# One table set for Ln and Exp, y normalised by ScalarE, and a new issue order in the six local-attention layers of a Trainium2 kernel

## The chip, the cores and the metric

The kernel runs on one core of a Trainium2 chip. The metric is device time in microseconds (us) of one execution. The engines are named as in the profile: PE is TensorE (PEld its weight loads), ACT is ScalarE, DVE is VectorE, POOL is GpSimd and SP is SyncE, which issues the DMAs.

## What is computed

Two blocks, each with a residual, on x of shape (4, 1024, 128). The first is causal attention with relative positions (16 heads of 8). The second, to which the change belongs, is six layers of local attention and a gated feed-forward net. In outline (shift_tokens moves half of the channels down by one token; a layernorm stands around each block):

```python
def attn_layer(x, Wqkv, qs, ksc, Wo):
    q, k, v = split_heads(x @ Wqkv)                 # 16 heads of 64
    q, k = l2norm(q) * qs, l2norm(k) * ksc
    q, k = rotary(q, k)                             # tables of cos and sin, times a scale
    out = local_attention(q, k, v)                  # windows of 32: own and the one before, softmax
    return out @ Wo

def ffn_layer(x, g, bln, W1, b1, W2, b2):
    xn = (x - mu) / sqrt(var + 1e-5) * g + bln
    a, gate = split(xn @ W1 + b1)                   # 341 columns each
    return a * gelu(gate) @ W2 + b2

for i in range(6):
    x = attn_layer(shift_tokens(x), ...) + x
    x = ffn_layer(shift_tokens(x), ...) + x
```

## The kernel before, in words

`build` runs five parts, one after the other: `first_projections`, `first_attention`, `first_output`, `layers` and `last_output`. Only `layers` changes. It treats the 4096 tokens as 32 tiles of 128 tokens; six layers make 192 tiles (TILES), numbered n, and m is the place of a tile in a ring of 8. Every engine has its own program: a function `body(t)` that lists the operations of that engine in the order of issue, where `for n, m in t.back(5)` names the tile that is five tiles behind the newest. So one body is a software pipeline over seven tiles, written out by hand. `rounds` writes the first 8 bodies out, then a loop (Fori) of 23 turns with 8 bodies in each, then the bodies that drain the pipeline (DEEPEST of them). Engines wait for each other by semaphores (a Mark each), and each engine issues strictly in its own order, so what is queued behind a waiting instruction waits too.

The work of one tile, by the engine that does it (lines are those of the kernel before):

- POOL copies the tile of x (`x_copied`, L964), PE turns it (`turn_x`, L1317), ACT copies it out of PSUM (`x_turned`, L1188 and L1189).
- PE computes q, k and v in six matmuls of 512 columns (`qkv`, L1328) into two PSUM banks in turn. Of the four pieces of q and k, ACT takes squares (`squared`, L1194), DVE sums them (`squares`, L1060) and multiplies with the rotary tables (`turned`, L1053); the two of v are copied by ACT (`v_out`, L1201).
- The l2 norm: DVE clips the sums (`clipped`, L1066), ACT guesses 1/sqrt as exp(-0.5 ln(s)) (`guess`, L1207 the Ln, L1209 the Exp), POOL makes one Newton step (`newton`, L984 to L990) and scales (`scaled`, L995), after it added the two halves of the rotation (`added`, L978 and L979).
- PE transposes q and k (`turn_q` L1336, `turn_k` L1343), ACT copies them out (`q_turned` L1216 and L1217, `k_turned` L1226), in two halves each. PE makes the scores (L1361), DVE subtracts the maximum, ACT takes the exponential (`exp`, L1231), DVE sums and normalises, PE transposes (`turn_p`, L1369), ACT copies out (`p_turned`, L1237 and L1238), PE multiplies with v (`values`, L1384) and ACT copies out (`o_out`, L1243).
- `out_proj` (PE, L1392), `with_x` (DVE), a shift by a DMA (`y_shifted`), `stats` (DVE), the root by POOL (`root`, L119), then `one`: DVE subtracts the mean and multiplies with 1/std (L124). PE turns the result (`turn_y`, L1398), ACT copies it out with gain and bias (`y_turned`, L1249).
- The feed-forward net runs once for two tiles, in bodies with an odd place: for each of three pieces PE computes value and gate (`hidden`, L1410), ACT the gelu of 256 columns (`gelu`, L1256), DVE the product (`gated`, L1115). Then `back_out` (PE, L1420) and `next_x` (DVE).

ScalarE computes Ln, Exp and Gelu from tables. Copy, Square and Identity are in every set of tables. The builder puts a table load (ACT_TABLE_LOAD) in front of a function that the set loaded last does not hold: in the kernel before these are in front of the Ln (L1207), the Exp of the guess (L1209), the first Gelu after an Exp (L1256) and the first Exp after a Gelu (L1231). A load that the program asks for itself stays where it is written.

Of the kernel before, what the change touches and what calls it, by code (L numbers as in the profile page):

```python
# [8 lines left out]
ALU = mybir.AluOpType  # L9
# [25 lines left out]
EPS = 1e-5  # L35
TILES = DEPTH * NT
# [4 lines left out]
DEEPEST = 7  # L41
# [773 lines left out]
def layers(nc, a, X, ident):  # L815

    with Part(nc, "la") as t:
# [19 lines left out]
        oT, yn, ynT = t.sb("oT", [P, 8, P]), t.sb("yn", [P, E]), t.sb("ynT", [P, 2, 2 * P])  # L837
        Y, yb = t.sb("Y", [P, TB + 1, 3 * (E // 2)]), t.sb("yb", [P, 4, E])
# [19 lines left out]
        wo_mm, y_ev, yn_ev, nT_mm, nT_ev, yb_ev = (mark(n) for n in ("wom", "ye", "yn", "ntm", "nte", "yb"))  # L858
# [26 lines left out]
        def _(e):  # L885
# [46 lines left out]
            def body(t):  # L932
                for n, m in t.back(7):
                    next_layer(n, m)
                for n, m in t.back(6):
                    w1_in(n, m)
                for n, m in t.back(5):
                    y_shifted(n, m)
                for n, m in t.back(3):
                    v_shifted(n, m)  # L940
# [5 lines left out]
        def _(e):  # L946
# [69 lines left out]
            def body(t):  # L1016
                for n, m in t.back(0):
                    x_copied(n, m)
                for n, m in t.back(1):
                    table(n, m)  # L1020
                for n, m in t.back(4):
                    added(n, m, 0)
                    added(n, m, 1)
                    carried(n, m)
                    newton(n, m)
                for n, m in t.back(6):
                    with_b2(n, m)
                for n, m in t.back(4):
                    scaled(n, m, 0)
                for n, m in t.back(6):  # L1030
                    root(n, m)
                for n, m in t.back(4):
                    scaled(n, m, 1)
# [3 lines left out]
        def _(e):  # L1037
            for mark in (x_ev, ss_ev, rot_ev, cl_ev, sub_ev, nm_ev, y_ev, yn_ev, a_ev, c_mx, c_sum, c_rc):
                mark.open(e)
# [85 lines left out]
            def body(t):  # L1125
                for n, m in t.back(5):
                    over_sum(n, m, 0)
                    normal(n, m, 0)
                    largest(n, m, 1)
                    below(n, m, 1)  # L1130
                for n, m in t.back(6):
                    stats(n, m)
                for n, m in t.back(3):
                    turned(n, m, 0)
                for n, m in t.back(7):
                    if m % 2:
                        gated(n, m, 2)
                for n, m in t.back(5):
                    summed(n, m, 1)
                for n, m in t.back(6):  # L1140
                    one(n, m)
                for n, m in t.back(3):
                    squares(n, m, 0)
                    turned(n, m, 1)
                for n, m in t.back(5):
                    over_sum(n, m, 1)
                    normal(n, m, 1)
                for n, m in t.back(3):
                    squares(n, m, 1)
                    turned(n, m, 2)  # L1150
                for n, m in t.back(4):
                    largest(n, m, 0)
                for n, m in t.back(6):
                    if m % 2:
                        gated(n, m, 0)
                for n, m in t.back(3):
                    turned(n, m, 3)
                for n, m in t.back(4):
                    below(n, m, 0)
                for n, m in t.back(3):  # L1160
                    squares(n, m, 3)
                    squares(n, m, 2)
                    clipped(n, m)
                for n, m in t.back(6):
                    if m % 2:
                        gated(n, m, 1)
                for n, m in t.back(4):
                    summed(n, m, 0)
                for n, m in t.back(7):
                    if m % 2:  # L1170
                        next_x(n, m)
                for n, m in t.back(5):
                    with_x(n, m)
# [3 lines left out]
        def _(e):  # L1177
            for mark in (xT_ev, sq_ev, v_ev, r_ev, c_ln, Tq_ev, Tk_ev, ex_ev, pt_ev, o_ev, nT_ev, g_ev):
# [66 lines left out]

            def y_turned(n, m):
# [12 lines left out]
            def body(t):  # L1259
                for n, m in t.back(7):  # L1260
                    if m % 2:
                        gelu(n, m, 2)
                for n, m in t.back(5):
                    exp(n, m, 1)
                for n, m in t.back(0):
                    x_turned(n, m)
                for n, m in t.back(3):
                    squared(n, m, 1)
                for n, m in t.back(5):
                    p_turned(n, m, 0)  # L1270
                for n, m in t.back(4):
                    q_turned(n, m, 0)
                for n, m in t.back(6):
                    y_turned(n, m)
                for n, m in t.back(5):
                    o_out(n, m, 0)
                for n, m in t.back(4):
                    k_turned(n, m, 0)
                for n, m in t.back(3):
                    squared(n, m, 2)  # L1280
                for n, m in t.back(5):
                    p_turned(n, m, 1)
                for n, m in t.back(3):
                    squared(n, m, 3)
                for n, m in t.back(6):
                    if m % 2:
                        gelu(n, m, 0)
                for n, m in t.back(4):
                    q_turned(n, m, 1)
                for n, m in t.back(5):  # L1290
                    o_out(n, m, 1)
                for n, m in t.back(3):
                    v_out(n, m, 4)
                for n, m in t.back(6):
                    if m % 2:
                        gelu(n, m, 1)
                for n, m in t.back(4):
                    exp(n, m, 0)
                    k_turned(n, m, 1)
                for n, m in t.back(3):  # L1300
# [7 lines left out]
        def _(e):  # L1308
# [115 lines left out]
            def body(t):  # L1424
                for n, m in t.back(0):
# [4 lines left out]
                for n, m in t.back(3):  # L1430
                    qkv(n, m, 1)
                for n, m in t.back(4):
                    e.wait_ge(Tk_ev.sem, Tk_ev.v(n - 1, 2))
                    e.wait_ge(Tq_ev.sem, Tq_ev.v(n - 1, 2))
                    turn_q(n, m, 0)
                for n, m in t.back(3):
                    qkv(n, m, 2)
                for n, m in t.back(7):
                    if m % 2:
                        back_out(n, m)  # L1440
                for n, m in t.back(6):
                    e.wait_ge(xT_ev.sem, xT_ev.v(upto(n + 6)))
# [3 lines left out]
                for n, m in t.back(5):  # L1446
                    e.wait_ge(pt_ev.sem, pt_ev.v(n, 1))
                    e.wait_ge(o_ev.sem, o_ev.v(n - 1, 2))
                    values(n, m, 0)
                for n, m in t.back(4):  # L1450
                    e.wait_ge(Tq_ev.sem, Tq_ev.v(n, 1))
                    e.wait_ge(Tk_ev.sem, Tk_ev.v(n - 1, 2))
                    turn_k(n, m, 0)
                for n, m in t.back(3):
                    qkv(n, m, 3)
                for n, m in t.back(5):
                    e.wait_ge(o_ev.sem, o_ev.v(n, 1))
                    e.wait_ge(pt_ev.sem, pt_ev.v(n, 1))
                    turn_p(n, m, 1)
                for n, m in t.back(6):  # L1460
                    if m % 2:
                        hidden(n, m, 0)
                for n, m in t.back(4):
                    e.wait_ge(Tk_ev.sem, Tk_ev.v(n, 1))
                    e.wait_ge(Tq_ev.sem, Tq_ev.v(n, 1))
                    turn_q(n, m, 1)
                    scores(n, m, 0)
                for n, m in t.back(5):
# [3 lines left out]
                for n, m in t.back(3):  # L1472
                    qkv(n, m, 4)
                for n, m in t.back(6):
# [158 lines left out]
```

## Time and profile before

| | |
|---|---|
| time, median of 3 runs | 5648.67 us (5640.5 to 5655.38) |
| the profiled execution's own time | 5650.0 us |
| its span in the profile | 5648.2 us |
| PE busy (matmuls) | 4771.1 us, 84% |
| ACT busy | 4267.2 us, 76% |
| DVE busy | 3970.2 us, 70% |
| POOL busy | 2332.2 us, 41% |
| mean granted TensorE clock | 0.948 of full speed |

Busy time is the time in which an engine has at least one instruction under way; the span is that of the profiled execution from its first to its last instruction. Shares are averages over parts of the program that differ: the layers take some seven tenths of the span.

### The profile page before, as it was taken

The numbers are of one execution on the slowest core, as the hardware profiler recorded it, in microseconds if no ns is written. First come the engines' busy times: TensorE is split into PE (matmuls) and PEld (weight loads), VectorE is DVE, ScalarE is ACT, GpSimd is POOL, SyncE is SP. The second block draws the span as 40 slices with busy tenths as digits, with TensorE's granted clock in tenths as the row PEclk, the third lists the DMA queues.
The fourth block names the chain that finished last, engine by engine and source line by source line (L and its number), as shares of the span: only waits on it lengthen the run. The fifth ranks groups of instructions, "written<-read, shape, count | busy, mean of one in ns | idle before, by whom it ended". The sixth has DMA issues, their size and how long they took to land. (4 is left out here: it accounts for less than half of the span.)

```text
span 5648.2 us, 139360 instructions
## 1 busy us (share of the span) xinstructions
PE 4771.1 (84%) x44000; PEld 3074.7 (54%) x44000; DVE 3970.2 (70%) x9123; ACT 4267.2 (76%) x7350; POOL 2332.2 (41%) x2840
## 2 busy tenths in 40 slices
PE   4999999999588888888888888888888888888884
PEld 2444444444355665556565655666556556665563
DVE  5666666656677777777777777777777777777774
ACT  1555555555288888888888888888888888888883
POOL 0000000000255555555555555555555555555552
PEclk6999999999699999999999999999999999999996
DMA  6444444444111111111111111111111111111111
GB/s 218 144 135 145 138 145 145 132 138 143 65 37 37 37 28 34 37 37 33 37 36 32 31 37 37 37 34 31 34 37 33 37 37 36 27 35 37 37 36 39
DMA packets 258979, 361.58 MB, mean 64 GB/s; under 512 B 44404, under 2 KB 216156, under 8 KB 257884
## 3 DMA queue, kind: packets, MB, share of 16 engines
q1 hardware_dynamic: 258140, 351.55, 20.3%
q8 instruction: 386, 6.32, 0.5%
q14 instruction: 453, 3.71, 0.2%
HBM read 151.19 MB, written 93.34 MB: 43 GB/s over the span
## 5 line engine op out<-in xcount | busy, mean ns | idle before, releaser
L1328 PE MATMUL la_ps<-la_Wqkv,la_xsT 128*128 (+1 forms) x2304 | 1278.8, 638 | 4.6 <-ACT la_v L1201 2.2
L995 POOL TENSOR_TENSOR la_rt<-la_rt,la_rn 128x1024 f32<-128x1024 f32 x384 | 729.8, 1901 | 0.3
L635 PE MATMUL at_ps<-at_pT,at_vh 128*32 128x512 f32 (+3 forms) x1536 | 596.5, 511 | 28.6 <-DVE at_pT L479 20.4
L1053 DVE TENSOR_TENSOR la_rsk<-la_ps,la_tab 128x1024 f32<-128x1024 f32 x384 | 468.4, 1220 | 212.2 <-ACT la_sq L1194 211.7
L978 POOL TENSOR_TENSOR la_rt<-la_rsq 128x512 f32<-128x512 f32 x192 | 245.2, 1277 | 848.4 <-PE la_ps L1336 843.7
L445 POOL COPY at_vh<-V 128x64 f32 (+1 forms) x64 | 15.0, 237 | 1272.1 <-PE at_ps L635 1272.0
L1336 PE MATMUL la_ps<-ident,la_rt 128*128 128x128 f32 x1536 | 249.8, 288 | 308.2 <-POOL la_rt L995 308.2
L1194 ACT ACTIVATE la_sq<-la_ps 128x512 f32<-128x512 f32 x768 | 456.8, 595 | 63.7 <-PE la_ps L1328 53.9
L1060 DVE TENSOR_REDUCE la_ssum<-la_sq 128x8 f32<-128x512 f32 x768 | 502.6, 675 | 0.0
L1053 DVE TENSOR_TENSOR la_rsq<-la_ps,la_tab 128x1024 f32<-128x1024 f32 x384 | 467.6, 1218 | 47.8 <-ACT la_sq L1194 20.9
L1361 PEld LDWEIGHTS la_ps<-la_kT,la_qB 128*64 128x64 f32 x12288 | 389.3, 138 | 145.1 <-issue 145.1
L1073 DVE TENSOR_REDUCE la_rmax<-la_ps 128x8 f32<-128x512 f32 x384 | 265.4, 691 | 282.0 <-PE la_ps L1361 282.0
L1336 PEld LDWEIGHTS la_ps<-ident,la_rt 128*128 128x128 f32 x1536 | 185.8, 147 | 479.1 <-issue 466.4
L622 PEld LDWEIGHTS at_ps<-ident,at_probs 128*128 128x128 f32 x2304 | 278.9, 147 | 300.8 <-issue 160.2
L1361 PE MATMUL la_ps<-la_kT,la_qB 128*64 128x64 f32 x12288 | 442.4, 225 | 0.0
L1384 PE MATMUL la_ps<-la_pB,la_vs 128*64 128x64 f32 x6144 | 390.4, 226 | 38.3 <-ACT la_pB L1238 28.5
L550 ACT ACTIVATE at_pT<-at_ps 128x512 f32<-128x512 f32 (+1 forms) x384 | 200.3, 522 | 293.4 <-PE at_ps L622 211.7
L479 DVE COPY at_pT<-at_ps 128x384 f32<-128x384 f32 (+2 forms) x384 | 196.7, 512 | 296.9 <-PE at_ps L635 296.1
L622 PE MATMUL at_ps<-ident,at_probs 128*128 128x128 f32 x2304 | 379.6, 289 | 15.0 <-DVE at_pT L479 15.0
L1328 PEld LDWEIGHTS la_ps<-la_Wqkv,la_xsT 128*128 128x128 f32 x2304 | 360.8, 197 | 42.8 <-issue 7.1
L1392 PE MATMUL la_ps<-la_Wo,la_oT 128*128 (+1 forms) x3072 | 382.2, 278 | 0.9 <-ACT la_oT L1243 0.9
L1384 PE MATMUL la_ps<-la_pB,la_v 128*64 128x64 f32 x6144 | 381.5, 223 | 0.0
(168 smaller groups left out, 11666.4 us busy)
## 6 DMA issues: line engine op xcount, KB each, us to landing
at_band<-skew_scratch SPq DMA_DIRECT2D x64, 1536.0 KB, 7.3
la_vs<-la_v SPq DMA_DIRECT2D x192, 384.0 KB, 3.5
skew_scratch<-at_R SPq DMA_DIRECT2D x64, 1024.0 KB, 5.3
la_vs<-la_v SPq DMA_DIRECT2D x192, 128.0 KB, 3.6
la_Wqkv<-in_wqkv SPq DMA_DIRECT2D x28, 384.0 KB, 4.9
kt_scratch<-pr_k SPq DMA_DIRECT2D x24, 384.0 KB, 2.9
qt_scratch<-pr_q SPq DMA_DIRECT2D x24, 384.0 KB, 3.4
at_qh<-qt_scratch SPq DMA_DIRECT2D x64, 144.0 KB
```

Of the source, the lines that this page charges most:

```text
L622: mm = e.transpose(ps[:, T_BANKS[jj % 2], i % G * P:(i % G + 1) * P], probs[u][:, m % 2, i % G, j * P:(j + 1) * P], ident[:])
L635: e.matmul(ps[WIN * c:WIN * (c + 1), O_BANK, c0:G * P], vh[:, m, j, :], pT[:, jj % 2, c0:G * P], start=(j < G), stop=(j >= G * u), skip_gr ...
L995: e.tensor_tensor(heads(rt, w), heads(rt, w), wide(rn[:, w * H:(w + 1) * H], D), ALU.mult)\
L1053: e.tensor_tensor(dst.rearrange("p f (h d) -> p f h d", d=D), ps[:, c % 2, :].rearrange("p (h d) -> p h d", d=D).unsqueeze(1).to_broadcast ...
L1060: e.tensor_reduce(ssum[:, c * 8:(c + 1) * 8], sq[:, c % 2, :].rearrange("p (h d) -> p h d", d=D), AX.X, ALU.add).then_inc(ss_ev.sem, 1)
L1073: e.tensor_reduce(rmax[:, h, :], windows(h), AX.X, ALU.max).then_inc(c_mx.sem, 1)
L1194: e.activation(sq[:, c % 2, :], ps[:, c % 2, :], ACT.Square).then_inc(sq_ev.sem, 1)
L1328: e.matmul(ps[:, c % 2, :], xsT[:, m * P:(m + 1) * P], Wqkv[:, ds(layer(n) % 2, 1), c * 512:(c + 1) * 512], start=True, stop=True)\
L1336: mm = e.transpose(ps[:, BANK_T, j * P:(j + 1) * P], rt[:, c:c + P], ident[:])
L1361: mm = e.matmul(bank[g * D:(g + 1) * D, col:col + D], qB[:, 4 * h + j, w, :, :], kT[:, 4 * h + j, at:at + 2 * WIN], start=False, stop=True ...
L1384: mm = e.matmul(to[:, :, g, :], keys[:, head:head + D], pB[:, pair, 2 * g + par, :, :], start=True, stop=True, skip_group_check=True)
L1392: mm = e.matmul(ps[:, BANK_Y, 0:E], oT[:, j, :], Wo[:, ds(layer(n) % 2, 1), j, :], start=(j == 0), stop=(j == 7))
```

## The change

It has six parts, all in `layers`.

1. `e.preload_act_table_set("natural_log_exp_and_others")` is called once ahead of the loop of ScalarE and at seven places of each body. This set holds Ln and Exp.
2. `one` moves from DVE to ACT, as an Identity with scale 1/std and bias -mean/std. DVE computes this bias in `mean_over`, one column wide.
3. `stats` waits for `yn_ev` of the tile before, since ACT now reads what `stats` overwrites.
4. The pipeline is one tile deeper: DEEPEST is 8, `one` and `y_turned` run 7 tiles back, the gelus 8, and most other lags grow by one.
5. The order of the bodies of all five engines is new.
6. On ACT the three gelus of a pair are in one body, with other work between them.

```diff
+LN_AND_EXP = "natural_log_exp_and_others"
...
-DEEPEST = 7
+DEEPEST = 8
...
             def stats(n, m):
...
+                e.wait_ge(yn_ev.sem, yn_ev.v(n - 1))
                 ln.take(e, [Y[:, m, 0:E]], n)
 
-            def one(n, m):
+            def mean_over(n, m):
+
                 e.wait_ge(ln.rstd.sem, ln.rstd.v(n))
-                e.wait_ge(nT_mm.sem, nT_mm.v(n - 1))
-                ln.one(e, 0, Y[:, m, 0:E], yn[:]).then_inc(yn_ev.sem, 1)
+                e.scalar_tensor_tensor(nmr[:], ln.st[:, 0, 6:7], -1.0, ln.st[:, 0, 8:9], ALU.mult, ALU.mult)\
+                    .then_inc(nmr_ev.sem, 1)
...
         @block.scalar
...
+            e.preload_act_table_set(LN_AND_EXP)
...
+            def one(n, m):
+                e.wait_ge(nmr_ev.sem, nmr_ev.v(n))
+                e.wait_ge(nT_mm.sem, nT_mm.v(n - 1))
+                e.activation(yn[:], Y[:, m, 0:E], ACT.Identity, bias=nmr[:], scale=ln.st[:, 0, 8:9]).then_inc(yn_ev.sem, 1)
...
             def body(t):
+                for n, m in t.back(6):
+                    exp(n, m, 0)
                 for n, m in t.back(7):
+                    o_out(n, m, 1)
+                for n, m in t.back(8):
+                    if m % 2:
+                        gelu(n, m, 0)
+                for n, m in t.back(4):
+                    squared(n, m, 0)
+                for n, m in t.back(5):
+                    v_out(n, m, 5)
+                    e.preload_act_table_set(LN_AND_EXP)
+                for n, m in t.back(8):
+                    if m % 2:
+                        gelu(n, m, 1)
+                for n, m in t.back(5):
+                    q_turned(n, m, 0)
...
+                for n, m in t.back(8):
                     if m % 2:
                         gelu(n, m, 2)
                 for n, m in t.back(5):
+                    k_turned(n, m, 0)
+                for n, m in t.back(6):
                     exp(n, m, 1)
-                for n, m in t.back(0):
+                for n, m in t.back(5):
+                    q_turned(n, m, 1)
+                for n, m in t.back(1):
                     x_turned(n, m)
...
+                    e.preload_act_table_set(LN_AND_EXP)
+                for n, m in t.back(4):
+                    squared(n, m, 3)
+                    e.preload_act_table_set(LN_AND_EXP)
+                for n, m in t.back(6):
+                    o_out(n, m, 0)
+                for n, m in t.back(7):
+                    one(n, m)
+                    e.preload_act_table_set(LN_AND_EXP)
+                for n, m in t.back(4):
+                    v_out(n, m, 4)
+                    e.preload_act_table_set(LN_AND_EXP)
                 for n, m in t.back(5):
+                    k_turned(n, m, 1)
+                for n, m in t.back(7):
+                    y_turned(n, m)
+                    e.preload_act_table_set(LN_AND_EXP)
                 for n, m in t.back(6):
...
+                for n, m in t.back(4):
                     guess(n, m)
-                    v_out(n, m, 5)
-                for n, m in t.back(2):
-                    squared(n, m, 0)
+                    e.preload_act_table_set(LN_AND_EXP)
```

PE's new body begins with `qkv` of piece 0, `out_proj`, `hidden` of piece 1, `turn_q` of half 0, `qkv` of piece 1, and has `values` of half 0, `turn_q` of half 1, `turn_x`, `back_out` in its middle and `values` of half 1, `hidden` of piece 0 at its end. POOL copies x first and normalises (`newton`, both `scaled`) ahead of the adds.

What ScalarE is given to do shows in three places of its program, inside the loop. The first is the guess near the end of a body, before the change (`la_lns` is the logarithm, `la_r` the guess):

```order
L1231 ACTIVATE la_ps<-la_ps 128x512
L1226 ACTIVATE la_kT<-la_ps 128x4x128
L1205 REGISTER_ALU
L1207 ACT_TABLE_LOAD
L1207 ACTIVATE la_lns<-la_hs 128x32
L1209 ACT_TABLE_LOAD
L1209 ACTIVATE la_r<-la_lns 128x32
L1197 REGISTER_ALU
L1201 ACTIVATE la_v<-la_ps 128x512
```

and the same place of the changed kernel:

```order
L1256 ACTIVATE la_ynT<-la_ps,la_lnb,la_lng 128x128
L1317 ACT_TABLE_LOAD
L1239 ACTIVATE la_pB<-la_ps 64x16x32
L1240 ACTIVATE la_pB<-la_ps 64x16x32
L1207 REGISTER_ALU
L1209 ACTIVATE la_lns<-la_hs 128x32
L1211 ACTIVATE la_r<-la_lns 128x32
L1322 ACT_TABLE_LOAD
L1233 ACTIVATE la_ps<-la_ps 128x512
```

The two loads in front of Ln and Exp are gone, and two that the program asks for (L1317, L1322) stand around the pair.

The second is the middle of the body of an even tile in the changed kernel, which has no gelu (`la_yn` is the normalised y):

```order
L1301 ACT_TABLE_LOAD
L1194 REGISTER_ALU
L1195 REGISTER_ALU
L1196 ACTIVATE la_sq<-la_ps 128x512
L1304 ACT_TABLE_LOAD
L1245 ACTIVATE la_oT<-la_ps 128x512
L1251 ACTIVATE la_yn<-la_Y,la_nmr,la_ln_stats 128x128
L1309 ACT_TABLE_LOAD
L1199 REGISTER_ALU
L1202 ISA
L1203 ACTIVATE la_v<-la_ps 128x512
L1312 ACT_TABLE_LOAD
```

Four loads stand among copies and squares, where the kernel before has none; the seventh of such a body, L1278, follows `v_out`.

The third is the start of the body of an odd tile in the changed kernel, with its gelus (`la_gl`):

```order
L1263 ACT_TABLE_LOAD
L1263 ACTIVATE la_gl<-la_ps,la_b 128x256
L1194 ISA
L1195 REGISTER_ALU
L1196 ACTIVATE la_sq<-la_ps 128x512
L1199 REGISTER_ALU
L1203 ACTIVATE la_v<-la_ps 128x512
L1278 ACT_TABLE_LOAD
L1261 REGISTER_ALU
L1262 REGISTER_ALU
L1263 ISA
L1263 ACT_TABLE_LOAD
```

The load at L1278 takes the gelu set away, so the second gelu has a load of its own. In such a body one more load (L1233) stands ahead of `exp` after the third gelu.

## Rows read from the trace of the kernel before

**Rows 1.** The page: span, and busy time, share and instructions of each engine.

```profile
span 5648.2 us, 139360 instructions
PE 4771.1 (84%) x44000; PEld 3074.7 (54%) x44000; DVE 3970.2 (70%) x9123; ACT 4267.2 (76%) x7350; POOL 2332.2 (41%) x2840
```

**Rows 2.** Busy time by stretch: stretch, us, then PE, PEld, DVE, ACT, POOL, clock, DMA.

```profile
2500.00:3500.00 1000.00, 856.01 (x9401) 603.67 (x9402) 747.39 (x1338) 872.54 (x1459) 563.26 (x674) 0.97 0.12 34
```

**Rows 3.** Groups of ACT, the whole span: busy us, mean ns | idle before.

```profile
L1207 ACT ACT_TABLE_LOAD x192 | 246.3, 1283 | 3.4
L1209 ACT ACT_TABLE_LOAD x192 | 246.3, 1283 | 3.4
L1256 ACT ACT_TABLE_LOAD x191 | 245.1, 1283 | 42.6 <-issue 39.6
L1231 ACT ACT_TABLE_LOAD x190 | 243.8, 1283 | 3.4
```

**Rows 4.** Timeline of ACT: start us, duration us, what.

```profile
3515.29 0.47 ACT L1256 ACTIVATE la_gl<-la_ps,la_b 128x256 f32<-128x256 f32 x1
3515.78 1.28 ACT L1231 ACT_TABLE_LOAD   x1
3517.07 0.58 ACT L1231 ACTIVATE la_ps<-la_ps 128x512 f32<-128x512 f32 x1
3517.57 0.59 ACT L1226 ACTIVATE la_kT<-la_ps 128x512 f32<-128x512 f32 x1
3518.18 1.28 ACT L1207 ACT_TABLE_LOAD   x1
3519.47 0.23 ACT L1207 ACTIVATE la_lns<-la_hs 128x32 f32<-128x32 f32 x1
```

**Rows 5.** Groups in 2500 to 3500 us: a load, y_turned, one.

```profile
L1207 ACT ACT_TABLE_LOAD x48 | 61.6, 1283 | 0.9
L1249 ACT ACTIVATE la_ynT<-la_ps,la_lnb,la_lng 128x128 f32<-128x128 f32 x48 | 22.0, 457 | 41.2 <-PE la_ps L1398 40.8
L124 DVE TENSOR_SCALAR la_yn<-la_Y,la_ln_stats 128x128 f32<-128x128 f32 x48 | 55.1, 1148 | 0.0
```

**Rows 6.** Waits in 2500 to 3500 us: total us, times, longest.

```profile
PE la_ps L1336 <- POOL la_rt L995: 75.7, 42, 2.0
PE la_ps L1317 <- POOL la_xc L964: 29.9, 6, 5.0
PE la_ps L1398 <- DVE la_yn L124: 23.0, 24, 1.0
ACT L1256 <- issue: 10.7, 6, 1.9
ACT la_gl L1256 <- issue: 9.1, 6, 1.6
```

**Rows 7.** Timeline: from a copy of ACT to PE, and three batches of PE.

```profile
3527.45 0.59 ACT L1238 ACTIVATE la_pB<-la_ps 64x512 f32<-64x512 f32 x1
...
3528.45 0.34 PE L1384 MATMUL la_ps<-la_pB,la_vs 128*64 128x64 f32 x4 [0.49 <-ACT la_pB L1238]
...
3531.32 0.60 PE L1336 MATMUL la_ps<-ident,la_rt 128*128 128x128 f32 x4
...
3535.48 1.95 PE L1392 MATMUL la_ps<-la_Wo,la_oT 128*128 x16
```

**Rows 8.** Timeline of PE, one batch at both clocks, and a stretch as in rows 2.

```profile
5546.64 1.09 PE L1336 MATMUL la_ps<-ident,la_rt 128*128 128x128 f32 x4 [3.47 <-POOL la_rt L995]
...
5553.53 0.60 PE L1336 MATMUL la_ps<-ident,la_rt 128*128 128x128 f32 x4
...
5560.00:5580.00 20.00, 13.66 (x138) 11.76 (x138) 6.47 (x18) 8.19 (x13) 1.01 (x3) 0.74 0.01 2
```

**Rows 9.** Timeline of PE: the first and the last batch of the layers.

```profile
1551.52 0.45 PE L1317 MATMUL la_ps<-ident,la_xc 128*128 128x128 f32 x1 [23.14 <-POOL la_xc L964]
...
5595.78 2.93 PE L1420 MATMUL la_ps<-la_W,la_gT 128*128 128x128 f32 x12 [1.08 <-DVE la_gT L1115]
```

More of the change, by code:

```diff
@@ L1018, in body @@
                     x_copied(n, m)
[L1019 removed]
+                for n, m in t.back(5):
+                    newton(n, m)
+                    scaled(n, m, 0)
+                    scaled(n, m, 1)
+                for n, m in t.back(7):
+                    with_b2(n, m)
+                    root(n, m)
+                for n, m in t.back(5):
+                    carried(n, m)
+                for n, m in t.back(3):
                     table(n, m)
@@ L1037, in _ @@
         def _(e):
-            for mark in (x_ev, ss_ev, rot_ev, cl_ev, sub_ev, nm_ev, y_ev, yn_ev, a_ev, c_mx, c_sum, c_rc):
+            for mark in (x_ev, ss_ev, rot_ev, cl_ev, sub_ev, nm_ev, y_ev, nmr_ev, a_ev, c_mx, c_sum, c_rc):
                 mark.open(e)
@@ L1125, in body @@
             def body(t):
[L1126 to L1133, printed above, removed]
-                    turned(n, m, 0)
[L1135 to L1164, printed above, removed]
+                for n, m in t.back(4):
+                    squares(n, m, 0)
+                for n, m in t.back(7):
+                    with_x(n, m)
+                for n, m in t.back(4):
+                    turned(n, m, 0)
+                for n, m in t.back(8):
                     if m % 2:
@@ L1167, in body @@
                 for n, m in t.back(4):
-                    summed(n, m, 0)
+                    turned(n, m, 1)
+                for n, m in t.back(7):
+                    stats(n, m)
+                for n, m in t.back(8):
+                    if m % 2:
+                        gated(n, m, 2)
+                for n, m in t.back(4):
+                    turned(n, m, 2)
+                    squares(n, m, 1)
+                    squares(n, m, 2)
+                for n, m in t.back(6):
+                    summed(n, m, 1)
+                    over_sum(n, m, 1)
+                for n, m in t.back(7):
+                    mean_over(n, m)
+                for n, m in t.back(6):
+                    normal(n, m, 1)
+                for n, m in t.back(4):
+                    turned(n, m, 3)
+                    squares(n, m, 3)
+                for n, m in t.back(5):
+                    largest(n, m, 0)
+                for n, m in t.back(4):
+                    clipped(n, m)
+                for n, m in t.back(5):
+                    below(n, m, 0)
+                    largest(n, m, 1)
+                    summed(n, m, 0)
+                    over_sum(n, m, 0)
+                    below(n, m, 1)
+                    normal(n, m, 0)
+                for n, m in t.back(8):
+                    if m % 2:
+                        next_x(n, m)
                 for n, m in t.back(7):
                     if m % 2:
-                        next_x(n, m)
-                for n, m in t.back(5):
-                    with_x(n, m)
+                        gated(n, m, 0)
             rounds(e, body, TILES, TB, DEEPEST)
@@ L1177, in _ @@
         def _(e):
-            for mark in (xT_ev, sq_ev, v_ev, r_ev, c_ln, Tq_ev, Tk_ev, ex_ev, pt_ev, o_ev, nT_ev, g_ev):
+            for mark in (xT_ev, sq_ev, v_ev, r_ev, c_ln, Tq_ev, Tk_ev, ex_ev, pt_ev, o_ev, yn_ev, nT_ev, g_ev):
                 mark.open(e)
@@ L1271, in body @@
-                for n, m in t.back(4):
[L1272 to L1299, printed above, removed]
@@ L1424, in body @@
             def body(t):
-                for n, m in t.back(0):
+                for n, m in t.back(4):
+                    qkv(n, m, 0)
+                for n, m in t.back(7):
+                    e.wait_ge(nT_ev.sem, nT_ev.v(n - 1))
+                    e.wait_ge(xT_ev.sem, xT_ev.v(upto(n + 5)))
+                    e.wait_ge(y_ev.sem, y_ev.v(n - 1))
+                    out_proj(n, m)
+                for n, m in t.back(8):
+                    if m % 2:
+                        hidden(n, m, 1)
+                for n, m in t.back(5):
+                    e.wait_ge(Tk_ev.sem, Tk_ev.v(n - 1, 2))
+                    e.wait_ge(Tq_ev.sem, Tq_ev.v(n - 1, 2))
+                    turn_q(n, m, 0)
+                for n, m in t.back(4):
+                    qkv(n, m, 1)
+                for n, m in t.back(6):
+                    e.wait_ge(o_ev.sem, o_ev.v(n - 1, 2))
+                    e.wait_ge(pt_ev.sem, pt_ev.v(n - 1, 2))
+                    turn_p(n, m, 0)
+                for n, m in t.back(4):
+                    qkv(n, m, 2)
+                for n, m in t.back(5):
+                    e.wait_ge(Tq_ev.sem, Tq_ev.v(n, 1))
+                    e.wait_ge(Tk_ev.sem, Tk_ev.v(n - 1, 2))
+                    turn_k(n, m, 0)
+                for n, m in t.back(8):
+                    if m % 2:
+                        hidden(n, m, 2)
+                for n, m in t.back(6):
+                    e.wait_ge(pt_ev.sem, pt_ev.v(n, 1))
+                    e.wait_ge(o_ev.sem, o_ev.v(n - 1, 2))
+                    values(n, m, 0)
+                for n, m in t.back(5):
+                    e.wait_ge(Tk_ev.sem, Tk_ev.v(n, 1))
+                    e.wait_ge(Tq_ev.sem, Tq_ev.v(n, 1))
+                    turn_q(n, m, 1)
+                for n, m in t.back(1):
                     e.wait_ge(y_ev.sem, y_ev.v(n - 6))
@@ L1429, in body @@
                     turn_x(n, m)
[L1430 to L1438, printed above, removed]
+                for n, m in t.back(8):
                     if m % 2:
                         back_out(n, m)
+                for n, m in t.back(4):
+                    qkv(n, m, 3)
+                for n, m in t.back(5):
+                    scores(n, m, 0)
+                    e.wait_ge(Tq_ev.sem, Tq_ev.v(n, 2))
+                    e.wait_ge(Tk_ev.sem, Tk_ev.v(n, 1))
+                    turn_k(n, m, 1)
+                for n, m in t.back(4):
+                    qkv(n, m, 4)
                 for n, m in t.back(6):
+                    e.wait_ge(o_ev.sem, o_ev.v(n, 1))
+                    e.wait_ge(pt_ev.sem, pt_ev.v(n, 1))
+                    turn_p(n, m, 1)
+                for n, m in t.back(7):
                     e.wait_ge(xT_ev.sem, xT_ev.v(upto(n + 6)))
```

97 lines of the change are left out of this document (31 added, 66 removed).

## The prediction

> **What bounds the kernel now.** I read the page first. It puts PE at 84%, ACT at 76% and DVE at 70% of a span of 5648.2 us [rows 1], which alone would say that PE is the bound and that ACT has a quarter of the time left. The change touches only the layers, so I asked the trace for a stretch inside them. There the picture differs: in 1000 us PE is busy 856.01 us and ACT 872.54 us [rows 2]. ACT is the fullest engine of the part that is changed, not PE. The stretch holds 48 tiles, since one load at L1207 belongs to each tile and there are 48 [rows 5]; a tile takes 1000/48 = 20.83 us. PE works 17.83 of them, ACT 18.18. The layers last from PE's first transpose at 1551.5 to the end of its last batch at 5595.78 + 2.93 = 5598.7 [rows 9], which is 4047 us: 192 tiles at 20.83 us are 4000, and 47 are filling and draining.
>
> Then I asked what ACT is busy with. Four groups of table loads, of 190 to 192 each and 1283 ns each, take 981 us together [rows 3]; that is 4 x 1.283 = 5.13 us of a tile. The other 18.18 - 5.13 = 13.05 us are copies, squares and functions. In the waits of the stretch, PE waits for POOL's scaling 75.7 us, for the copy of x 29.9 us and for `one` on DVE 23.0 us [rows 6]. The first of these stands behind the guess with its two loads. So loads on ACT sit on the chain that paces a tile.
>
> **The change part by part, in us per tile.**
>
> Table loads. This is the term that decides, and it comes out of the order, not out of the words of the change. Sharing one set removes the two loads at L1207 and L1209: -2 x 1.283 = -2.57. But the order of the changed kernel has a load at each of the seven places where the program asks for one, in every body, although nothing between them has changed the set: only copies, squares, Identity, Ln and Exp lie there. A body of an odd tile has three more: two for gelus, because the load at L1278 stands between them, and one for the Exp after the third. So two tiles have 7 + 10 = 17 loads, where before they had 8. That is 8.5 a tile. All loads of the trace take 1283 ns, but each of them changes the set, so the trace does not show what a load of the set already loaded costs. The bounds are 0 and 1.283. I take 1.283, because four groups at four places, towards three kinds of function, have the same mean to the nanosecond [rows 3]: the time doesn't look at what is loaded, and it would be odd if it looked at what was there. At that price the loads are 8.5 x 1.283 = 10.91 a tile, 5.78 more than now.
>
> The Trainium skill bears on this in "ScalarE: Activation LUTs", What ACT_TABLE_LOAD costs: the load takes about 1283 ns for every set, because the whole slot is copied. By this a load of the same set would cost the same; no row of the trace can say so. The same section adds a drain of some 1380 ns to a switch. Here the trace disagrees: the Exp starts at 3517.07, and the load before it ended at 3515.78 + 1.28 = 3517.06 [rows 4]. By the page's 2.66 us the sum below would end at some 8950 us; the trace decides, and I leave the drain out.
>
> The neighbours of a load. Two neighbouring copies overlap: one starts at 3517.07 and takes 0.58, the next starts at 3517.57 already. With a load between, the load waits for the copy's end (3517.57 + 0.59 = 3518.16, load at 3518.18) [rows 4]. So an added load also costs about 0.12 of overlap and gap: 4.5 more loads a tile, 0.54.
>
> `one` on ACT. It has the form of `y_turned` (Identity, bias and scale from columns, 128 by 128), 457 ns [rows 5]: +0.46. DVE loses an instruction of 1148 ns and gets one of a single column, so it is relieved by nearly 1 us; DVE is 75% busy in the stretch [rows 2], and its relief is worth nothing to an ACT that is never idle. The wait of `stats` for `yn_ev` can hold DVE only if ACT is a whole tile behind with `one`, which lies in ACT's body after DVE's `stats` of that tile; there are some 20 us between two such pairs. Nothing.
>
> The floor of ACT: 13.05 + 10.91 + 0.54 + 0.46 = 24.96. To this come small gaps of about 0.02 between some 25 instructions whose successors don't overlap: half a dozen of them a tile, 0.2 with register instructions, my estimate from the 0.9 us in 48 tiles of one such group [rows 5] times a dozen. ACT also stands still at each turn of the loop: two waits for "issue", 10.7 + 9.1 us in 6 turns [rows 6], 0.41 a tile. They stay, and as ACT is now the bound they count in full. 25.6.
>
> Round trips that ACT must still wait for. Where ACT hands a copy to PE and soon needs the result, the gap from the end of the copy to PE's start is 0.4 (3527.45 + 0.59 to 3528.45), and four transposes take 0.60 [rows 7]. Two such trips are short in the new order. `k_turned` of half 0 to `q_turned` of half 1 is 1.1, with only `exp` (0.5) between: 0.6 in even bodies; in odd ones a load fills it. `o_out` of half 1 to `q_turned` of half 0 goes through `out_proj`, 1.95 [rows 7], and four transposes: 0.4 + 1.95 + 0.6 = 2.95, against a square, a copy and a load, 2.3: 0.65 in even bodies, nothing in odd ones. Together 1.25 in every second body, 0.65 a tile. All other trips of the order have two loads or more between their ends. So a tile takes 25.6 + 0.65 = about 26.3.
>
> The new order on PE, POOL and SP. It moves the copy of x one body ahead of its transpose, which takes away up to 29.9/48 = 0.6, and with the shorter guess the 75.7/48 = 1.6 in front of `turn_q` [rows 6]. These are gains on PE's side. PE needs 17.83, DVE 15.6, POOL 11.7 of a tile [rows 2]; with ACT at 26.3 the gains turn into idle time of PE and are worth nothing. They would count if the loads cost nothing.
>
> Depth. One more tile in the pipeline lengthens filling and draining: between 0 and one body; I take 10 us, since the extra bodies are nearly empty.
>
> The sum, against the profiled execution (5650.0 us; the median of the runs is 5648.67, so both bases agree): 1551.5 before the layers, 192 x 26.3 = 5050, 47 + 10 for filling and draining, and 5650.0 - 5598.7 = 51 behind. This is 6710 us, 1060 us or 19% **slower**.
>
> **The rivals.**
>
> A, the forecast: every load costs 1.283 us, ACT is the bound. 6710 us; its own range goes from the floor of 24.96 without any wait (1551.5 + 4792 + 57 + 51 = 6450) to 28.8 (7190), where PE, with a third of its time idle, gets the lower clock for part of it and makes the round trips longer.
>
> B, a load of the set already loaded costs next to nothing. Then only the four loads of a pair that change the set count: ACT needs 13.05 + 0.46 + 2 x 1.283 = 16.1, less than PE's 17.83. PE is the bound, and of its 3.0 us of idle time the 1.6, the 0.6 and 0.5 (`one`, 23.0/48) are attacked by the shorter guess and the new order. If two thirds of this is got, a tile takes 19.0: 1551.5 + 3648 + 57 + 51 = 5310 us, faster by 6%. The turning point between A and B is a price of the 6.5 redundant loads of a tile at which ACT reaches the present 20.83: (20.83 - 16.1 - 1.3)/6.5, about 0.5 us each. For B speaks that such loads never occurred in the trace. Against it speaks that the four means are equal [rows 3]. The Trainium skill, same page and section, speaks of its price "for every switch to a different set", which read narrowly is this rival.
>
> C, PE gets the lower clock throughout. After an idle time of 3.47 us a batch of four transposes took 1.09 where it takes 0.60 otherwise, and a stretch in which PE was busy 68% had a clock of 0.74 of full speed, a mix of 2.4 and 1.2 GHz [rows 8]. In A, PE would be busy some 17.83/26.3 = 68%. Were all of it at 1.2 GHz, PE would need 17.83 x 1.09/0.60 = 32.4 a tile and be the bound: 1551.5 + 6221 + 108 = 7880 us. Against it: PE's work comes in dense parts of several us, and even the stretch quoted had half of its time at the full clock. A part of C lies inside A's range.
>
> D, the loads don't run as the order shows them. Only the row of the changed profile can tell; it ends as B.
>
> **How the numbers follow.** A has 0.81, B with D 0.14, C 0.04; 0.01 is for no difference, within 0.3%, about what a measurement of this kernel can tell. The predicted time is A's. The range, 6400 to 7250 us, takes A's bounds and some 50 us on either side for the small gaps and the clock; it leaves out B and most of C, about 0.2. Slower by over 0.3% is A and C, 0.85; faster 0.14.
>
> **What would show it.** In the changed profile, seven groups of table loads of about 192 each at L1278, L1301, L1304, L1309, L1312, L1317 and L1322, nearly 288 more at L1263 and L1233, all at 1283 ns and some 2090 us in total; ACT over 92% busy in the layers; a tile at about 26.3 us; PE busy about two thirds and waiting for ACT. If the groups at those seven lines have a mean far below 1283 ns, or are not there, A is wrong and B holds. If they are there at 1283 ns and a tile takes much more than 27 us, look at PE's clock (C) and at the two round trips.

## The result, and the profile after

The changed kernel takes 6793.2 us (median of 4 runs, 6783.64 to 6808.32) against 5644.59 us before: a ratio of 1.204, 95% interval 1.200 to 1.207. It is 20% slower. The forecast was 6710 us, with a range of 6400 to 7250.

The page of the changed kernel, as [rows 1]:

```profile
span 6787.4 us, 140579 instructions
PE 5209.6 (77%) x44000; PEld 3281.0 (48%) x44000; DVE 3795.7 (56%) x9123; ACT 5493.5 (81%) x8407; POOL 2342.7 (35%) x2840
```

ACT has gained 1226 us of busy time and is now ahead of PE. A stretch inside the layers, columns as in [rows 2]:

```profile
3500.00:4500.00 1000.00, 750.67 (x7242) 508.91 (x7241) 544.71 (x1037) 910.14 (x1332) 440.04 (x526) 0.87 0.10 27
```

ACT is busy 91%, PE 75%, and the granted clock fell from 0.97 to 0.87 of full speed. The groups of ACT over the whole span say what the time went into, as [rows 3]:

```profile
L1301 ACT ACT_TABLE_LOAD x192 | 246.3, 1283 | 3.4
L1304 ACT ACT_TABLE_LOAD x192 | 246.3, 1283 | 3.5
L1312 ACT ACT_TABLE_LOAD x192 | 246.3, 1283 | 3.4
L1322 ACT ACT_TABLE_LOAD x192 | 246.3, 1283 | 3.4
L1278 ACT ACT_TABLE_LOAD x192 | 246.3, 1283 | 3.4
L1309 ACT ACT_TABLE_LOAD x192 | 246.3, 1283 | 3.4
L1317 ACT ACT_TABLE_LOAD x192 | 246.3, 1283 | 3.4
L1263 ACT ACT_TABLE_LOAD x190 | 243.8, 1283 | 57.6 <-PE la_ps L1428 57.1
...
L1233 ACT ACT_TABLE_LOAD x95 | 121.9, 1283 | 1.7
```

All seven loads that the program asks for ran 192 times, each at 1283 ns. At L1304, L1309, L1312, L1317 and L1322 the set asked for is always there already; at L1278, in bodies with a gelu, it has to be brought back, and at L1301 it may have to be in the same bodies, behind the load for the Exp (L1233). With the two groups placed by the builder that is 2090 us of loads, where the kernel before has 981. Of the loads before, the two in front of the Ln and the Exp of the guess are gone.

One of these lines over 2500 to 5500 us, with the shortest, median and longest duration in ns and the first and last start:

```profile
L1304 ACT ACT_TABLE_LOAD  x112: 1283/1283/1283, 2503.4 to 5490.9; - x112
```

There is one such load a tile, so a tile takes (5490.9 - 2503.4)/111 = 26.9 us. The layers, from the first transpose to the last batch of PE, last from 1544.45 to 6737.54, or 5193 us (4047 before): 192 tiles at 26.91 us are 5167, and 26 are left for filling and draining.

What PE waits for, in the stretch from 3500 to 4500 us (total us, times, longest), and what ACT waits for:

```profile
PE la_ps L1373 <- issue: 107.7, 31, 3.5
PE la_ps L1387 <- ACT la_oT L1245: 66.7, 37, 2.0
PE la_ps L1373 <- ACT la_kT L1228: 20.8, 6, 3.5
```

```profile
ACT la_sq L1196 <- PE la_ps L1346: 24.4, 19, 4.1
ACT la_oT L1245 <- PE la_ps L1402: 19.1, 22, 1.3
ACT la_qB L1218 <- PE la_ps L1354: 13.2, 21, 1.4
ACT L1263 <- PE la_ps L1428: 11.2, 18, 0.6
ACT la_ps L1233 <- issue: 5.5, 5, 1.2
```

The timeline of PE shows what one of these does (start us, duration us):

```profile
3499.91 0.28 PE L1416 MATMUL la_ps<-ident,la_yn 128*128 128x128 f32 x1
3503.67 0.58 PE L1373 MATMUL la_ps<-la_mask,la_identb 128*128 128x512 bf16 x1 [3.47 <-issue]
3504.18 1.98 PE L1379 MATMUL la_ps<-la_kT,la_qB 128*64 128x64 f32 x32
3506.09 2.08 PE L1346 MATMUL la_ps<-la_Wqkv,la_xsT 128*128 x2
3508.09 0.48 PE L1402 MATMUL la_ps<-la_pB,la_vs 128*64 128x64 f32 x4
...
3509.95 1.12 PE L1346 MATMUL la_ps<-la_Wqkv,la_xsT 128*128 x2
```

PE comes to `scores` of half 1 and stands still for 3.47 us. The profile calls it "issue", since `scores` waits for several marks; in 6 cases it names `k_turned` (L1228), which in ACT's program stands behind the loads L1304, L1309 and L1312. After the idle time the same `qkv` takes 2.08 us, a little later 1.12: the batches between run at the lower clock. The stretches behind the idle time and after it, columns as in [rows 2], say the same of the granted clock:

```profile
3503.60:3509.90 6.30, 6.23 (x67) 4.19 (x67) 1.69 (x4) 5.11 (x8) 2.50 (x5) 0.50 0.00 0
3511.00:3520.00 9.00, 8.50 (x81) 6.00 (x82) 6.01 (x12) 8.09 (x14) 3.35 (x5) 1.00 0.23 65
```

The slow batches end in `values` of half 1, for which ACT waits at `o_out` (L1245, 19.1 us).

### The profile page after: what moved, and what is told of

Same layout as the page of the kernel before. It is cut to its first block and busy times, and to the rows that moved or that the text cites. A ratio compares the mean times of both kernels' runs of the same rounds, so it can differ in the third digit from the quotient of the medians.

```text
span 6787.4 us, 140579 instructions
## 1 busy us (share of the span) xinstructions
PE 5209.6 (77%) x44000; PEld 3281.0 (48%) x44000; DVE 3795.7 (56%) x9123; ACT 5493.5 (81%) x8407; POOL 2342.7 (35%) x2840
## 5 line engine op out<-in xcount | busy, mean ns | idle before, releaser
L1346 PE MATMUL la_ps<-la_Wqkv,la_xsT 128*128 (+1 forms) x2304 | 1369.8, 680 | 108.2 <-issue 76.3
L1373 PE MATMUL la_ps<-la_mask,la_identb 128*128 128x512 bf16 x384 | 183.5, 478 | 663.7 <-issue 564.9
L1379 PEld LDWEIGHTS la_ps<-la_kT,la_qB 128*64 128x64 f32 x12288 | 535.8, 180 | 205.2 <-issue 205.2
L1379 PE MATMUL la_ps<-la_kT,la_qB 128*64 128x64 f32 x12288 | 598.1, 271 | 0.0
L1402 PEld LDWEIGHTS la_ps<-la_pB,la_vs 128*64 128x64 f32 x6144 | 349.8, 153 | 397.2 <-issue 384.5
L1402 PE MATMUL la_ps<-la_pB,la_vs 128*64 128x64 f32 x6144 | 446.9, 245 | 84.1 <-ACT la_pB L1240 68.8
L1387 PE MATMUL la_ps<-ident,la_pr 128*128 128x128 f32 x1536 | 241.1, 280 | 339.1 <-ACT la_oT L1245 338.5
L1082 DVE TENSOR_REDUCE la_rs<-la_ps 128x8 f32<-128x512 f32 x384 | 263.1, 685 | 401.1 <-ACT la_ps L1233 401.1
L1387 PEld LDWEIGHTS la_ps<-ident,la_pr 128*128 128x128 f32 x1536 | 176.5, 141 | 596.7 <-ACT la_oT L1245 495.6
L1410 PEld LDWEIGHTS la_ps<-la_Wo,la_oT 128*128 128x128 f32 x3072 | 375.5, 195 | 118.1 <-issue 116.8
```

Source lines behind the costliest of these rows:

```text
L1082: e.tensor_reduce(rs[:, h, :], windows(h), AX.X, ALU.add).then_inc(c_sum.sem, 1)
L1346: e.matmul(ps[:, c % 2, :], xsT[:, m * P:(m + 1) * P], Wqkv[:, ds(layer(n) % 2, 1), c * 512:(c + 1) * 512], start=True, stop=True)\
L1379: mm = e.matmul(bank[g * D:(g + 1) * D, col:col + D], qB[:, 4 * h + j, w, :, :], kT[:, 4 * h + j, at:at + 2 * WIN], start=False, stop=True ...
L1387: mm = e.transpose(ps[:, BANK_P, j * P:(j + 1) * P], pr[:, h, j * P:(j + 1) * P], ident[:])
L1402: mm = e.matmul(to[:, :, g, :], keys[:, head:head + D], pB[:, pair, 2 * g + par, :, :], start=True, stop=True, skip_group_check=True)
L1410: mm = e.matmul(ps[:, BANK_Y, 0:E], oT[:, j, :], Wo[:, ds(layer(n) % 2, 1), j, :], start=(j == 0), stop=(j == 7))
```

## The experiments

Twelve kernels in four groups (e1 to e4, e5 to e8, e9 and e10, e11 and e12), each group with its own runs of the kernel before beside it; medians in us, ratios to the kernel before with 95% intervals. Where kernels of different groups are compared, I take the difference of their ratios times 5650 us; by the intervals such a difference is good to some 15 to 30 us.

| run | loads a tile | us | ratio |
|---|---|---|---|
| the change | 8.5 | 6793 | 1.204 (1.200 to 1.207) |
| e1, new order, loads only where the set changes | 1 | 5558 | 0.983 (0.982 to 0.985) |
| e2, e1 with three loads a body | 4 | 5999 | 1.060 (1.058 to 1.063) |
| e6, e1 with 2.5 loads at ACT's waits | 3.5 | 5709 | 1.009 (1.007 to 1.011) |
| e3, order of before, shared set | 2 | 5524 | 0.977 (0.975 to 0.978) |
| e4, e3 with seven redundant loads a body | 9.5 | 6710 | 1.187 (1.185 to 1.189) |
| e5, the change with two loads moved | 8.5 | 6722 | 1.188 (1.184 to 1.191) |
| e7, the change with `one` on DVE | 8.5 | 6670 | 1.180 (1.177 to 1.182) |
| e8, e1 with `one` on DVE | 1 | 5562 | 0.983 (0.982 to 0.985) |
| e9, e3 with 16 bodies a turn | 2 | 5447 | 0.967 (0.965 to 0.969) |
| e10, e1 with 16 bodies a turn | 1 | 5466 | 0.971 (0.969 to 0.974) |
| e11, e3 with 48 bodies a turn | 2 | 5414 | 0.957 (0.956 to 0.959) |
| e12, e1 with 48 bodies a turn | 1 | 5427 | 0.960 (0.959 to 0.961) |

**e1: the redundant loads taken out.** All seven calls in the body go, and one comes behind the third gelu:

```diff
                     if m % 2:
                         gelu(n, m, 2)
+                        e.preload_act_table_set(LN_AND_EXP)
...
-                    e.preload_act_table_set(LN_AND_EXP)
```

> The changed kernel with its order kept and the seven asked-for loads of a body taken out; one is asked for behind the third gelu instead. One load a tile is left (two of a pair), where the changed kernel has 8.5. Theory (the loads are the whole loss): ACT falls from 24.5 busy of 26.8 us to 24.5 - 7.5 x 1.283 = 14.9 a tile, PE becomes the bound, a tile takes about 19 us, 5300 us in all. Rival (the new order or the normalisation on ACT costs time by itself): a tile stays above 20.8 us, over 5650 us in all.

Measured 5558 us. The loads are the whole loss and more: without them the changed kernel is 1.7% faster than the kernel before. Its trace has 96 loads in front of gelus and 96 behind them in the layers and none in front of a copy, a square or an Identity. But a tile takes about 20.2 us, not 19. Its stretch:

```profile
3500.00:4500.00 1000.00, 889.92 (x9701) 621.09 (x9696) 726.88 (x1380) 730.23 (x1406) 582.85 (x698) 0.99 0.13 35
```

PE is at 89%, and ACT, at 73%, waits for PE at five places (1.2 us a tile at `q_turned` alone); four of them:

```profile
ACT la_qB L1218 <- PE la_ps L1348: 57.4, 74, 2.7
ACT la_sq L1196 <- PE la_ps L1340: 44.8, 50, 3.4
ACT la_oT L1245 <- PE la_ps L1396: 42.7, 44, 1.2
ACT la_v L1203 <- PE la_ps L1340: 32.8, 25, 1.4
```

No engine is full; PE and ACT wait for each other in turns, in two fixed orders.

**e2: three loads put back**, behind `x_turned`, `one` and `y_turned`.

> As the first, with three of the seven redundant loads put back (behind x_turned, behind one, behind y_turned): 4 loads a tile, as many as the kernel before has. Theory (each load costs its 1.283 us wherever ACT is the bound): ACT busy 14.9 + 3.85 = 18.7, with waits about 20.5 a tile, 5600 us. If a redundant load cost a chain more than its own length, it would lie above 5750; if ACT had room for three loads beside PE, near the first run.

Measured 5999 us, far above my 5600: 576 loads cost 442 us, 0.77 each, although e1's ACT is idle 27% of the time. The expectation that ACT's idle time would swallow most of them fails. Idle time at one place does not pay for a load at another. PE's wait in front of `scores` shows one way in which they cost (first row e1, second row e2, both 3500 to 4500 us), and the clock of the stretch is 0.95, 0.99 in e1:

```profile
PE la_ps L1367 <- issue: 23.5, 44, 0.8
PE la_ps L1370 <- issue: 76.3, 44, 2.1
```

From e2 to the change, another 864 loads cost 0.1434 x 5650 = 810 us, 0.94 each. e2 also has as many loads a tile as the kernel before, 4, and takes 6% longer: at an equal number the new order with its places for the loads is the worse one.

**e6: loads where ACT waits.** The three places chosen are just ahead of waits of e1: behind `exp` of half 0, behind `one`, and behind `v_out` of piece 5 in bodies without gelu.

> The first run's kernel (one load a tile, 5557 us) with 2.5 redundant loads a tile at the places where its ACT waits over 1.2 us for PE: behind exp 0 (ahead of o_out 1), behind one (ahead of v_out 4), and in bodies without gelu behind v_out 5 (ahead of q_turned 0). Theory (a load costs nothing where ACT waits anyway, its full time elsewhere): less than 0.5 us each, 480 loads, under 5750 us. Rival (each load costs about 0.77 us, as the three of the second run did, wherever it stands): 5557 + 480 x 0.77 = 5930 us.

Measured 5709 us: by the ratios 0.0258 x 5650 = 146 us for 480 loads, 0.30 each, against 0.77 in e2. Place decides more than number: 2.5 loads a tile more than e1 cost 146 us, 3 loads more cost 442. The load behind `one` stands in both kernels, so the difference comes from the others.

**e3 and e4: the order of before.** e3 asks for the shared set behind the second and behind the third gelu and changes nothing else; e4 adds calls behind seven operations of each body.

```diff
                     if m % 2:
                         gelu(n, m, 1)
+                        e.preload_act_table_set(LN_AND_EXP)
```

> The kernel before in its own order, with only the shared set: one load asked for behind each group of gelus, none in front of Ln and Exp, 2 loads a tile instead of 4. Theory (the two loads of the guess stand on the chain that paces a tile): PE's 1.6 us a tile in front of turn_q goes, 19.3 us a tile, about 5350 us. Rival (the kernel before is bound by PE and its order, the loads are hidden): 5600 to 5650 us.

> The third with a redundant load behind each of seven operations a body, in the order of the kernel before: 9.5 loads a tile. Theory (loads, not the order): ACT busy 13.05 + 9.5 x 1.283 + 0.6 = 25.8, a tile 26.5 to 28 us, 6700 to 7000 us. Rival (the new order makes the loss): well below 6500 us.

e3 took 5524 us, 131 us less than the kernel before: less than half of some 305 us that the 1.6 us a tile in front of `turn_q` promised. The wait of PE for POOL's scaling [rows 6] is gone, and from 3500 to 4500 us another stands in its place, for DVE:

```profile
PE la_ps L1332 <- DVE la_rsq L1054: 63.4, 44, 2.6
PE la_ps L1388 <- ACT la_pB L1240: 14.9, 19, 0.9
```

e4 took 6710 us, as the theory had it: 1440 loads cost 1186 us, 0.82 each. In the new order the same number, from e1 to the change, costs 0.2205 x 5650 = 1246 us, 0.87 each. Both orders lose nearly alike by redundant loads, so the new order isn't the cause of the loss. It isn't quite free either: e4 has one load a tile more than the change and is still 1.7 points faster. With few loads the order of before is even the better one (e3 against e1: 0.977 against 0.983).

**e5: two loads moved** away from `k_turned`, the number kept:

```diff
                 for n, m in t.back(6):
                     exp(n, m, 0)
+                    e.preload_act_table_set(LN_AND_EXP)
...
                     squared(n, m, 3)
-                    e.preload_act_table_set(LN_AND_EXP)
...
                     v_out(n, m, 4)
-                    e.preload_act_table_set(LN_AND_EXP)
...
                     p_turned(n, m, 1)
+                    e.preload_act_table_set(LN_AND_EXP)
```

> The changed kernel with all its 8.5 loads a tile, but two of them moved: those behind squared 3 and behind v_out 4, which stand ahead of k_turned of half 1, now stand behind p_turned of half 1 and behind exp of half 0. In the changed kernel PE idles 3.5 us a tile for this k_turned and does the next qkv and values at the lower clock. Theory (the loads ahead of k_turned make the idle time that drops the clock, and the slow batches make ACT wait for o_out): the clock in the layers rises from 0.87 to 0.93 or more, ACT waits less, a tile falls from 26.8 to about 26.2 us, 6680 us. Rival (only the number of loads matters): 6790 us, clock unchanged.

Measured 6722 us; by the ratios 0.0160 x 5650 = 90 us less than the change with the same loads. In the traces a tile takes 26.5 us in place of 26.9. In the stretch from 3500 to 4500 us the clock is 0.91 instead of 0.87, and ACT's wait at `o_out` is gone; the one at `q_turned` grew in its place, and PE waits for `o_out` instead:

```profile
3500.00:4500.00 1000.00, 764.81 (x7369) 525.55 (x7368) 557.42 (x1057) 916.43 (x1356) 445.15 (x530) 0.91 0.10 28
```

```profile
ACT la_qB L1218 <- PE la_ps L1354: 40.8, 38, 2.8
ACT L1263 <- PE la_ps L1428: 12.3, 11, 2.0
ACT la_sq L1196 <- PE la_ps L1346: 9.2, 9, 1.8
ACT la_ps L1233 <- issue: 6.4, 5, 1.5
PE la_ps L1410 <- ACT la_oT L1245: 86.2, 32, 3.6
```

So the same two loads cost some 0.4 us a tile less at their new places. This doesn't show that PE's clock alone is worth that much: the places were changed in two ways at once. The loads no longer stand ahead of `k_turned`, and they now stand ahead of the `o_out` for which ACT waited, where e6 found a load to be cheap. ACT's four waits above sum to 68.7 us, its five in the change to 73.4. The clock rose less than the 0.93 expected; PE's new idle times of up to 3.6 us for `o_out` are a likely reason that no run tests.

**e7 and e8: `one` back on DVE**, in the change and in e1.

> The changed kernel with the normalisation of y back on DVE, in the place of the bias, all loads kept. Theory (ACT is the bound, one costs it its 0.48 us): a tile 26.3 instead of 26.8 us, about 6700 us. Rival (DVE's 1.15 us delay something on the way): 6790 us or more.

> The first run's kernel (one load a tile, 5557 us) with the normalisation of y back on DVE. If ACT's time matters there, up to 90 us faster, 5470 us. If DVE's matters, where PE waits for DVE and ACT in turns, up to 130 us slower, 5690 us. Neither engine is the bound, so I expect within 50 us of 5557.

e7 took 6670 us, by the ratios 0.0242 x 5650 = 137 us less than the change: 0.71 us a tile, more than the 0.48 of the instruction. Its wait at `o_out` fell from 19.1 to 5.6 us in 1000, 0.36 a tile, which would be more than the rest; how the two share the gain is not shown. e8 took 5562 us, the same as e1. Moving work from DVE to ACT costs where ACT is the bound and is worth nothing where neither is.

**e9 to e12: fewer turns of the loop.** In the traces the engines stand still for "issue" at each turn. More bodies a turn make turns rarer:

```diff
-            rounds(e, body, TILES, TB, DEEPEST)
+            rounds(e, body, TILES, TB, DEEPEST, 2 * TB)
```

Here `rounds` writes 2 * TB (later 6 * TB) bodies into the loop and counts the turns accordingly; places still run in a ring of 8.

> The third run's kernel (order of before, shared set, 2 loads a tile, 5524 us) with 16 bodies in a turn of the loops of layers instead of 8: 11 turns in place of 23. The engines stand still some 3.7 us at each turn (ACT waits for issue 22.4 us in 6 turns of the third run). If this lies on the chain, 12 turns fewer give up to 45 us: 5480 us. If the instructions of a longer body have to be fetched just the same and the turn is not what costs, 5524 us.

> The first run's kernel (new order, one load a tile, 5557 us) with 16 bodies in a turn. Its PE stands still about 4.0 us a turn (waits for issue at qkv, longest 4.0, once a turn). By the same reckoning up to 48 us less: 5510 us; or 5557 us if the turn is not what costs.

> The ninth run's kernel (order of before, shared set) with 48 bodies in a turn: 3 turns in place of 11. Twelve turns fewer gave 77 us (5524 to 5447), 6.4 us each. By this 8 fewer give 51 us: 5396 us. If a long body is no longer fetched ahead in time, no gain or a loss, 5450 us or more.

> The tenth run's kernel (new order, one load a tile, 5466 us) with 48 bodies in a turn. Twelve turns fewer gave 91 us, 7.6 each; 8 fewer give 61: 5406 us.

The medians of e9 and e10, 77 and 91 us below e3 and e1, are well past the 45 and 48 expected, but they come from different groups; by the ratios the gains are 56 and 68 us. By ratios, e3 to e9 to e11 goes 0.977, 0.967, 0.957, and e1 to e10 to e12 0.983, 0.971, 0.960. Twenty turns fewer are worth 0.0195 x 5650 = 110 us in one order and 0.0233 x 5650 = 132 us in the other, 5.5 to 6.6 us a turn. Each engine's own wait at a turn is shorter: 31.1 us in 9 turns on ACT in e3 (3.5 each), 22.3 in 5 in e9 (4.5 each).

```profile
POOL la_xc L965 <- issue: 31.7, 9, 3.8
ACT L1258 <- issue: 31.1, 9, 4.7
```

```profile
ACT L1259 <- issue: 22.3, 5, 4.8
```

(The first two rows are of e3, the third of e9, both from 3000 to 4500 us.) I read the difference as engines that stop one after the other and then wait for each other. The trace of the change has it so at a turn:

```profile
3563.07 0.58 ACT L1233 ACTIVATE la_ps<-la_ps 128x512 f32<-128x512 f32 x1 [1.01 <-issue]
3566.48 1.12 PE L1346 MATMUL la_ps<-la_Wqkv,la_xsT 128*128 x2 [3.82 <-issue]
3567.73 0.60 ACT L1196 ACTIVATE la_sq<-la_ps 128x512 f32<-128x512 f32 x1 [3.57 <-PE la_ps L1346]
```

ACT stands 1.01 us for its own next instruction and then 3.57 for PE, which stood 3.82 for its own. For e9 to e12 the reading is argued, not shown. e11 is the best version, 4.3% faster than the kernel before and 20% faster than the change.

## Why the prediction was right, and by how much it was off

- **The deciding term was right.** "I take 1.283": a load of the set already loaded takes 1283 ns like any other, 7 x 192 times. This is what the trace of before could not show. Rivals B and D are out, and so is C: the clock in the layers is 0.87, not 0.5, and the time 6793 us, not 7880.
- **ACT's work was right.** 13.05 + 10.91 + 0.46 = 24.42 us a tile; busy time in the stretch from 2500 to 6500 us is 3658 us of 4000, at 26.91 us a tile 24.6. Of the 0.54 for lost overlap on top of it 0.2 is left, so about 0.35 was too much. `one` took 483 ns instead of 457. ACT is busy 91%, a little under the 92 that I named as a sign, and PE 75% and not two thirds: its batches at the lower clock count as busy too.
- **The waits were too small.** I had 0.41 for the turn of the loop and 0.65 for two trips, 1.06 together; the five waits of ACT above are 73.4 us in 37.2 tiles, 1.97. The step that failed is the sentence that "all other trips of the order have two loads or more between their ends". It fails twice. By the order itself the trip from `p_turned` of half 1 through `values` to `o_out` of half 1 has only one load between its ends, L1322. And two loads are no protection: `values` stands in PE's order behind `scores` and `qkv`, which start when `k_turned` of half 1 is done. From there to `o_out` ACT has two loads, L1317 and L1322, and still waits 0.5 us a tile, where PE does `scores`, `qkv` and `values` at a clock of 0.50 after 3.5 us of idle time. I had costed PE's batches from rows at the full clock; the lower clock for a part of PE's time stood in A's range but not in its sum. What the clock alone costs is not shown: e5 wins some 0.4 us a tile, but by two changes at once. Also missing was the trip through `hidden` to the first gelu, 0.3, and the turn of the loop was 0.6 and not 0.41, since ACT's wait for PE comes on top of its own (22.5 us in 5 turns, from the timeline of ACT). Of the two trips that I did count, `k_turned` to `q_turned` waits the 0.6 in even bodies that I gave it; the one through `out_proj` costs nothing outside the turns of the loop.
- **The sum.** 26.9 against 26.3 us a tile is 117 us; filling and draining took 31 us less than my 57, and the part ahead of the layers 7 less. The profiled execution took 6789 us, 79 more than forecast. In a tile, 0.35 too much for overlap stands against 0.9 too little for waits and 0.1 for small gaps. So the price and the number of the loads were forecast, and that the sum came within 1.2% is in part luck, by errors that cancel.
- **The new order on PE and POOL "worth nothing" under A:** nearly so. e4 has the old order, one load a tile more and 1.7 points less time, so the new order gives no gain under A and may cost a little. But the price of 19.0 us a tile that I gave it under B was wrong. With the redundant loads gone, e1 stays at 20.2: PE's waits for POOL turn into waits of PE and ACT for each other.
- **The turning point of B**, 0.5 us a load, rested on ACT's idle time swallowing loads. e2 shows that it does not: already 0.77 us a load is lost with ACT at 82%.

## What to carry to other kernels

A table load asked for by the program is an instruction of 1.283 us wherever it stands, needed or not: read the order of the built program and count loads a tile before trusting the wish behind them. One call behind each gelu whose set has to change back gave 2%; with seven calls a body the kernel was 20% slower. In a pipeline whose engines all issue in fixed orders, idle time is only worth something at its own place: the same kind of load cost 0.30 us ahead of a wait and 0.77 elsewhere. Where loads made PE stand still for 3.5 us, the batches right behind ran at half the clock as well.

## What the runs showed of the hardware that I had not expected

- A load of the set already loaded is not shortened: 1283 ns, in every one of five groups of 192 that hold nothing else. This agrees with the Trainium skill, "ScalarE: Activation LUTs", What ACT_TABLE_LOAD costs, that the whole slot is copied; the drain that the same section adds does not show here either: in the trace of the change a load of 1.28 us starts at 3499.77, 0.02 us after the instruction before it ended, and the next one starts at 3501.06.
- A turn of a loop over bodies written out costs 5.5 to 6.6 us of the whole, though no wait of PE, ACT, DVE or POOL for "issue" at a turn is longer than 5.3 us in these traces. The forecast had counted 3.3 us a turn.
